# Inverse deviations of the norms taken by GpSimd as a power, in a conv, attention and expert-routing kernel

## What is computed

```python
def _gn(v, G=32, eps=1e-05):          # over pairs of channels and all pixels
    ...
    return ((g - m) / jnp.sqrt(s + eps)).reshape(v.shape)
def _ln_t(v, eps=1e-05):              # over the 64 channels of a token
    ...
    return (v - m) / jnp.sqrt(s + eps)
...
x = x + _L0_conv_ref(_gn(x), ...)     # depthwise 5x5 taps, 1x5 taps, correlations
t = _to_tokens(x)
t = t + _L1_attn_ref(_ln_t(t), ...)   # k features, k'v matrices, q features, denominators
t = t + _L1_ffn_ref(_ln_t(t), ...)    # softmax over tokens, 8 tokens per expert, gelu network
```

## Time and profile before

| | us |
|---|---|
| median of 3 runs | 4081.96 (4072.59 to 4082.1) |
| the profiled execution | 4079.0 |
| its span, first to last instruction | 4077.2 |
| PE, DVE, ACT, POOL busy | 3586.0, 2994.3, 1687.9, 1248.6 |

### The profile page before, as it was taken

How to read it: one execution, slowest core, us unless ns; L and a number is a source line. 1 busy time by engine, 2 the same in 40 slices (tenths; PEclk the granted TensorE clock), 3 DMA queues, 4 the chain that set the end, 5 groups by cost and what they waited for, 6 DMA issues and landing times.

```text
span 4077.2 us, 52073 instructions
## 1 busy us (share of the span) xinstructions
PE 3586.0 (88%) x17556; PEld 1798.3 (44%) x17556; DVE 2994.3 (73%) x3523; ACT 1687.9 (41%) x1798; POOL 1248.6 (31%) x1327
## 2 busy tenths in 40 slices
PE   4798998989889998989889899899989898899976
PEld 2344444444544444444444445344444444544453
DVE  6878876788677876788767886778767887548823
ACT  0145533455254534445434553445435554343310
POOL 1015620176013740156201760127501572011100
PEclk8899998999999998999989999999989999899967
DMA  1000000000000001000000000000010000100045
GB/s 47 17 1 1 1 17 25 1 1 1 25 17 1 1 1 41 1 1 1 17 25 1 1 1 25 17 1 1 1 41 1 1 1 16 30 1 1 1 116 200
DMA packets 18676, 70.96 MB, mean 17 GB/s; under 512 B 8781, under 2 KB 13421, under 8 KB 13485
## 3 DMA queue, kind: packets, MB, share of 16 engines
q1 hardware_dynamic: 18365, 67.10, 5.3%
HBM read 37.26 MB, written 29.84 MB: 16 GB/s over the span
## 4 chain that ended last, share of the span: by engine, by line
issue 48%; PE 33%; DVE 8%; POOL 7%; ACT 2%; DMA 1%; SPq 1%; POOLq 0%; DVEq 0%; ACTq 0%
PE ps_D L1499 11%; POOL UA L549 4%; PE ps_E L1463 4%; PE ps_C L1488 3%; PE ps_A L1446 3%; PE ps_B L1446 3%; DVE RR L1106 2%; PE ps_E L1474 1%; DVE region L1076 1%; DVE arena L911 1%; PE ps_C L1417 1%; POOL RS L581 1%; PE ps_E L1512 1%; POOL RR L574 1%; DVE region L1085 1%
## 5 line engine op out<-in xcount | busy, mean ns | idle before, releaser
L562 POOL TENSOR_TENSOR arena<-arena,UHL 128x896 f32<-128x896 f32 x350 | 764.6, 2210 | 226.3 <-ACT UHL L695 211.6
L1499 PE MATMUL ps_D<-region,small 128*128 128x448 f32 x1792 | 785.2, 562 | 32.9 <-DVE OS L1112 32.8
L549 POOL TENSOR_TENSOR UA<-region,CS 128x128 f32<-128x128 f32 (+1 forms) x400 | 178.8, 449 | 1837.8 <-DVE region L986 795.3
L1085 DVE TENSOR_TENSOR region<-region,ps_C 128x896 f32<-128x896 f32 x448 | 485.9, 1085 | 247.9 <-PE ps_C L1488 247.9
L1499 PEld LDWEIGHTS ps_D<-region,small 128*128 128x128 f32 x1792 | 321.2, 194 | 346.7 <-issue 284.8
L734 ACT ACTIVATE EQ<-ps_B,NEG 128x896 f32<-128x896 f32 x224 | 225.6, 1007 | 480.4 <-PE ps_B L1446 480.3
L911 DVE SCALAR_TENSOR_TENSOR arena<-arena,W8C 128x896 f32<-128x896 f32 (+1 forms) x418 | 416.8, 1010 | 1.2
L1417 PE MATMUL ps_C<-region,UA 128*128 128x512 f32 (+1 forms) x800 | 382.7, 601 | 2.9 <-ACT region L627 2.9
L734 ACT ACTIVATE EQ<-ps_A,NEG 128x896 f32<-128x896 f32 x224 | 225.6, 1007 | 350.8 <-PE ps_A L1446 350.7
L695 ACT ACTIVATE UHL<-arena,W8C 128x896 f32<-128x896 f32 x350 | 361.2, 1032 | 0.0
L1052 DVE SCALAR_TENSOR_TENSOR region<-region,ps_B 128x1024 f32<-128x1024 f32 (+1 forms) x200 | 243.9, 1219 | 159.8 <-ACT region L713 156.4
(11 more groups left out here) (310 smaller groups left out, 5772.9 us busy)
## 6 DMA issues: line engine op xcount, KB each, us to landing
arena<-x SPq DMA_DIRECT2D x8, 1568.0 KB, 6.6
t_keep<-Y SPq DMA_DIRECT2D x7, 1568.0 KB, 6.8
w_keep<-region SPq DMA_DIRECT2D x7, 784.0 KB, 5.7
CST<-t_keep SPq DMA_DIRECT2D x2, 1568.0 KB, 10.0
small<-t_keep SPq DMA_DIRECT2D x2, 1568.0 KB, 12.8
plane<-w_keep SPq DMA_DIRECT2D x4, 784.0 KB, 15.9
UHL<-t_keep SPq DMA_DIRECT2D x2, 1568.0 KB, 12.3
out<-CST SPq DMA_DIRECT2D x2, 1568.0 KB, 11.7
```

The source lines that it names most:

```text
L562: pool.tensor_tensor(out=X[:, cut], in0=X[:, cut], in1=PRODUCT[m % 3], op=ALU.add).then_inc(pool_taps.sem, 1)
L1085: dve.tensor_tensor(out=q, in0=q, op=ALU.mult, in1=here.area(key)[:, :].rearrange("p (c n) -> p c n", c=2)[:, :, 0:PIX])\
L1499: ins = pe.matmul(here.area(key)[:, 0:PIX], MW[i][:, c, :], Q[s % 3][:, c, :], start=c == 0, stop=c == NCHUNK - 1)
```

## The change

The power of minus one half of (variance + epsilon) takes the place of root and reciprocal. For each token group POOL does two instructions on 14 columns (`deviations`: multiply by 1/64 and add epsilon, then a power whose exponent is a column of -0.5), with a wait of its own between them. For the channel norm DVE adds epsilon out of PSUM at tile 16 (`SPREAD_TILE`), POOL takes the power of one column behind its `UA` of that tile, and `NORM_TILE` goes from 16 to 18. ACT's roots and DVE's reciprocals of deviations are gone (DVE's self-waits from 53 to 44 a pass), and with them all table loads but those of the first instruction and of the last function. Tiles are moved: the power for groups 2 and 3 at tiles 5 and 9, scaling at 7 and 11 (from 9 and 10), split at 8 and 12 (from 11 and 12), transposes at 11 and 15 (from 13 and 15). In the slots the scaling is seven slots behind `LN2_SLOTS` instead of six. POOL's part of the two groups in `back` stands at the end of its pass.

```diff
-STD_TILE = 8
-SCALE_TILES = [None, None, 9, 10]
-SPLIT_TILES = [None, None, 11, 12]
-UTS_TILES = [None, 2, 13, 15]
+STD_TILES = [None, None, 5, 9]
+SCALE_TILES = [None, None, 7, 11]
+SPLIT_TILES = [None, None, 8, 12]
+UTS_TILES = [None, 2, 11, 15]
...
-STATS_TILE, MEAN_TILE, CENTRE_TILE, VAR_TILE, NORM_TILE = 3, 12, 13, 15, 16
+STATS_TILE, MEAN_TILE, CENTRE_TILE, VAR_TILE, SPREAD_TILE, NORM_TILE = 3, 12, 13, 15, 16, 18
...
+            def deviations(sums, std, pair, g, turn):
+
+                pool.wait_ge(*sums.at(pair, g + 1))
+                passed(pool)
+                pool.tensor_scalar(ST[:, g % 2, 2, :], ST[:, g % 2, 1, :], 1.0 / C, LN_EPS, ALU.mult, ALU.add)\
+                    .then_inc(variance.sem, 1)
+                pool.wait_ge(*turn)
+                pool.tensor_tensor(out=ST[:, g % 2, 3, :], in0=ST[:, g % 2, 2, :], op=ALU.pow,
+                                   in1=NEGH[:, 0:1].broadcast_to([P, 2 * GROUP])).then_inc(std.sem, 1)
+
+            def group_norm(here):
+
+                pool.wait_ge(*here.emptied("gvar"))
+                pool.tensor_tensor(out=MV[:, 7:8], in0=MV[:, 6:7], in1=NEGH[:, 0:1], op=ALU.pow)\
+                    .then_inc(gn_scale.sem, 1)
...
+                    if k in STD_TILES:
+                        deviations(ln1_sums, ln1_std, pair, STD_TILES.index(k), variance.at(pair, STD_TILES.index(k) - 1))
+                    if here.span == "loop" and k == SPREAD_TILE:
+                        group_norm(here)
...
-
+                    if j - 5 in LN2_SLOTS:
+                        deviations(ln2_sums, ln2_std, pair, LN2_SLOTS[j - 5], variance.at(pair, 3 + LN2_SLOTS[j - 5]))
+                deviations(ln2_sums, ln2_std, pair, NG - 1, variance.at(pair, 2 + NG))
+                for g in range(2) if here.span == "loop" else ():
+                    deviations(ln1_sums, ln1_std, pair + 1, g, variance.at(pair, 3 + NG + g))
...
-            def deviations(sums, std, pair, g):
-                act.wait_ge(*sums.at(pair, g + 1))
-                act.activation(ST[:, g % 2, 2, :], ST[:, g % 2, 1, :], ACT.Sqrt, scale=1.0 / C,
-                               bias=EPS[:, 0:1])\
-                    .then_inc(std.sem, 1)
...
-                    if k == VAR_TILE and here.span == "loop":
-                        group_norm(here)
...
-            def group_norm_apply(here):
-                dve.wait_ge(*here.emptied("gvar"))
-                link(dve.reciprocal(MV[:, 7:8], MV[:, 6:7]))
+            def group_norm_spread(here):
+                dve.wait_ge(*here.filled("gvar"))
+                dve.tensor_scalar(MV[:, 6:7], here.area("gvar")[:, 0:1], GN_EPS, None, ALU.add)\
+                    .then_inc(*here.empty("gvar"))
+
+            def group_norm_apply(pair):
+                dve.wait_ge(*gn_scale.at(pair, 1))
...
                 dve.wait_ge(*std.at(pair, g + 1))
-                link(dve.reciprocal(st[:, 3], st[:, 2]))
...
-                    if j - 6 in LN2_SLOTS:
-                        norm_scale(2, ln2_std, pair, LN2_SLOTS[j - 6]).then_inc(un2_ready.sem, 1)
+                    if j - 7 in LN2_SLOTS:
+                        norm_scale(2, ln2_std, pair, LN2_SLOTS[j - 7]).then_inc(un2_ready.sem, 1)
```

More of the change, by code:

```diff
@@ L200, in program @@
         GBC = sb("GBC", [C, 1])
-        EPS = sb("EPS", [P, 1])
         NEG1 = sb("NEG1", [P, 1])
+        NEGH = sb("NEGH", [P, 1])
         BS = sb("BS", [P, NPIX, 6])
@@ L343, in program @@
         gn_mean = signal("gn_mean", 1)
+        gn_scale = signal("gn_scale", 1)
+        variance = signal("variance", 2 * NG, setup=2)
         g_ready = signal("g_ready", 1)
@@ L526, in _ @@
             pool.memset(SEL[:, :, :, :, :], 0.0)
-            pool.memset(EPS[:, :], GN_EPS)
             pool.memset(NEG1[:, :], -1.0)
+            pool.memset(NEGH[:, :], -0.5)
             pool.memset(BD[:, :, :], 0.0)
@@ L584, in split @@
                     passed(pool)
-                for j in range(SLOTS + POOL_LAG):
+                for j in range(ALL_SLOTS):
                     if slot_of_step(j, RECIP_LAG + 1):
@@ L590, in pair_of_images @@
                         tap_sum(j - POOL_LAG)
+                    if j - 5 in LN2_SLOTS:
[3 more added lines that the diff above has]
+                    deviations(ln1_sums, ln1_std, pair + 1, g, variance.at(pair, 3 + NG + g))
+            group_norm(Here("setup"))
+            for g in range(2):
+                deviations(ln1_sums, ln1_std, 0, g, variance.first(g + 1))
             with pool.Fori(0, PAIRS - 1) as pair:
@@ L602, in _ @@
             act.wait_ge(*loaded.first(1))
[L604 to L608, removed]
             def front(here, chunks):
@@ L676, in back @@
                         split_tokens(here, 0)
-                    deviations(ln1_sums, ln1_std, pair, g)
                     high_part(pair, g)
@@ L716, in pair_of_images @@
                         tokens(here, 1, YT_TILES.index(k))
-                    if k == STD_TILE:
-                        for g in (2, 3):
-                            deviations(ln1_sums, ln1_std, pair, g)
                     if k in SPLIT_TILES:
@@ L740, in pair_of_images @@
                         tokens(here, 2, LN2_SLOTS[j])
-                    if j - 5 in LN2_SLOTS:
-                        deviations(ln2_sums, ln2_std, pair, LN2_SLOTS[j - 5])
                     if here.span == "loop" and j in FRONT_SLOTS:
                         front(here, [FRONT_SLOTS[j]])
-                deviations(ln2_sums, ln2_std, pair, NG - 1)
                 for g, (t, m) in enumerate(GROUPS):
@@ L763, in _ @@
             act.wait_ge(*zeroed.first(2))
-            group_norm(start)
             front(start, range(NPIX))
@@ L1139, in pair_of_images @@
                         group_norm_variance(here)
+                    if conv and k == SPREAD_TILE:
+                        group_norm_spread(here)
                     if conv and k == NORM_TILE:
-                        group_norm_apply(here)
+                        group_norm_apply(pair + 1)
                     if conv and k > NORM_TILE:
@@ L1182, in _ @@
             group_norm_variance(start)
-            group_norm_apply(start)
+            group_norm_spread(start)
+            group_norm_apply(0)
             back(start, 0, None)
@@ L1623, in _ @@
                         .then_inc(*end.fill(key))
-VSETUP = 63
-VLOOP = 53
+VSETUP = 60
+VLOOP = 44
 LOW = -3.0e38
```

## The result

| | us |
|---|---|
| before, median of 20 runs | 4079.37 (4069.91 to 4083.7) |
| after, median of 20 runs | 4102.35 (4076.03 to 4104.87) |
| ratio after / before, 95% interval | 1.0037, 1.0023 to 1.0051 |
| ratio of the two medians | 1.0056 |

The forecast was 4069, faster. The median lies inside its range of 4044 to 4108, but the sign is wrong. The two ratios in the table differ because the runs of after lie in two groups and the median falls into the larger. There is nothing between the groups: 8 of 20 at 4076.0 to 4079.1, 12 at 4101.9 to 4104.9. The profiled execution of after (4104.4, span 4102.6) is one of the longer.

What follows compares the result with a forecast made beforehand. PE, busy 88% of the span, was taken as the bound, with ACT mattering only where PE or DVE waits. Terms -40 + 19 + 10 - 2 = -13 us against 4079.0 gave 4066, 4069 for the median; range 4044 to 4108.

Steps and rivals of the forecast that it cites:

- the price of the power: POOL's power on 14 columns in the token norms: taken as 0.7 us, between 0.1 and 2.21.
- a serial place: One of 24 norms with nothing beside them: 0.8 us more each (bounds 0.1 and 2.5), 19 us in all.
- Rival (a): Power is slow software and the 24 serial places decide: at 2.1 us a power, 53 us and 4103; chance 0.23.
- Rival (b): Power costs like a product, at most 0.2 us: 0.3 us a serial norm, 7 us, giving 4057; chance 0.17.
- The sign to look for: End of the back stage: 1.4 us from sum to scaling, not 0.64; PE's next-pass wait longer by twice the difference.
- The k tiles: PE's waits around tiles 9 to 19 go: gain of about 40 us (bounds 25 and 47).
- Rival (c): K tiles broken in a new place by DVE's backlog at tile 7 or tile 11's copies: 4085; chance 0.10.
- the transposes' new place: Transposes at tile 11 remove both waits before tile 14: 3.4 us in two passes, 4.2 in five, 1.6 in the last.
- the missing exchange: At tile 8, no more table loads and roots on ACT between two exponentials: gain of 0.8 us a pass.
- The rule on the table load: Skill's drain of about 1.38 us per ACT load, 2.66 in all: tile 8's exchange would be 5.8 us, not 3.13.
- The moved pieces: Two depthwise pieces a pass move from k tiles into q slots 35 and 36: 1.5 us in seven passes, 10 us lost.
- An unchanged q stage gives 10 us back.: Sign against the forecast: if the q slots do not lengthen, the 10 us charged for the moved depthwise pieces return.

Runs made afterwards that it cites:

- run 7: Changed kernel with POOL's two instructions on 8 columns instead of 14 for the last group: 4101.18 us, ratio 1.0019 to the kernel before.
- the long form: The slower of two groups of runs of the unaltered changed kernel: 12 of 20 at 4101.9 to 4104.9 us; its profiled execution took 4104.4.
- the short form: The faster group of runs of the unaltered changed kernel, 8 of 20 at 4076.0 to 4079.1 us; profiled once more at 4078.0, span 4076.1.
- run 3: Kernel before with only the change's new tile numbers, roots and reciprocals kept everywhere: 4035.42 us, ratio 0.9890.
- run 5: Changed kernel with the power on POOL everywhere but the old tile numbers (powers at tiles 5 and 8): 4119.54 us, ratio 1.0052 to the kernel before.
- run 6: Kernel before with DVE's depthwise pieces beginning two tiles later, so two pieces a pass move into the q slots: 4085.14 us, ratio 0.9985.
- the hybrid: Changed kernel with ACT's root and DVE's reciprocal back in the 24 serial places, POOL's power kept elsewhere: 4023.31 us, ratio 0.9862 to the kernel before.

## Why the prediction was wrong

**The step that failed is the price of the power.** "I take 0.7, half as much again as the 128-column row, which is the nearest in size." It is 2.58. The size of a tile was the wrong yardstick: the rows of POOL then at hand were sums, products and casts, where 896 columns took 2.21 us, 0.0025 a column; run 7 gives the power 0.16 a column. The upper bound, 2.21, was drawn from the same kind of row and was also too low. The other terms of the chain were near: hand-overs 0.3 for 0.5, scale and add 0.21 for 0.2. With 2.58 in place of 0.7 a serial place costs 2.46 by the trace, 24 of them 59 and not 19, and my sum would have read -40 + 59 + 10 - 2 = +27, 4109. By stages the 24 places cost 54 us where 19 were forecast. That takes back the whole gain of the k tiles and leaves the change at nothing; that the median is slower beyond this is a second term, the long form's clock in the back stage, which the sum had at nothing without a reason.

Rival (a), with its break-even at a power of about 1.2 us, was the mechanism; it had a chance of 0.23. That its 4103 meets the median is luck: the k tiles gave 9 us more than its sum has, the q slots were not longer, the power cost more still, and 26 us in the back stage belong to the clock; the short form lies at 4078. That the median lies inside the range is luck of the same kind. The range itself was not added up right: the terms of a serial place give 0.2 to 2.3 us and not 0.1 to 2.5, so 5 to 55 us, and ends of 4045 and 4105.

Rival (b) priced the power at 0.2 us at most, a thirteenth of what it took. The Trainium skill's rule beside it (GPSIMD Engine Reference, Performance versus the Vector engine: about twice VectorE's time for two-input operations, measured there on an add) does not carry over: for this operation the trace does not agree, 2.58 us against the 0.5 worked out from it. The sign to look for, PE's wait ahead of the next pass longer by twice the difference, was misplaced too: half of it fell on the wait for the low part of group 0, and of the other half 0.98 went into slower matmuls.

**The k tiles: right in mechanism, 9 us short.** Forecast -40, measured -48.7 (-45.3 in the short form). Exponential 14 comes 2.58 us after 13 and no PE wait is left at tiles 12 to 14. In pairs two and five of the loop, k tiles go from 147.1 to 142.0, 5.1 us for the 4.7 forecast. In the other five it is some 149.2 to 142.0, 7.2 for 5.5. Part of that difference is clock. Busy time in 3.4 us ahead of exponential 14, before, pair three and then pair two:

```profile
1178.90:1182.30 3.40, 3.04 (x6) 1.45 (x7) 0.00 (x0) 1.35 (x2) 0.00 (x0) 0.51 0.00 0
705.90:709.30 3.40, 3.40 (x13) 1.67 (x12) 1.22 (x1) 1.11 (x1) 0.40 (x1) 1.00 0.00 0
```

In pair two too PE had just stood idle, but its clock stayed; in the five other passes it fell to the lower level for 3.4 us (6.8 in the first). In after it doesn't do so anywhere between the first three k tiles and the q slots. I had read the 7.62 of the earlier trace rows as a longer wait. Rival (c), tiles broken in a new place, didn't come.

**Who earned it.** I ascribed most of the gain to the transposes' new place and 0.8 a pass to the missing exchange. Runs 3 and 5 bear that out from both sides. That most of the 50 us of loads had been hidden was right as well: ACT is 138 us less busy, and in run 5 the missing roots are worth about 0.9 us of a pass. The rule on the table load that the prediction cites from the Trainium skill (ScalarE: Activation LUTs, What ACT_TABLE_LOAD costs) does not agree with one more exchange either: 3.13 us from tiles 8 to 9 in the earlier trace rows, 2.92 in run 3 with one root (685.20 to 688.12), where the two loads alone would be 5.3 by it.

**The moved pieces: the local price right, its part in the whole not found.** 1.5 us was forecast for the four slots; 1.7 and 0.9 were measured, and the q slots of run 6 are 10.8 us longer. By its runs the kernel before gets no slower by it all the same; where the loss is made up is open.

**"An unchanged q stage gives 10 us back."** It came out at -5.3 in after and +1.2 in the short form.

**What the sum didn't contain.** The clock in the back stage, +25.9 in after and -9.5 in the short form, is as large as any term of mine. In the short form all terms are -45.3 (k), +1.2 (q), +17.2 (drain), -9.5 (back), +33.4 (residuals), +1.9 (setup), together -1.1, the measured 4076.1 - 4077.2.

**Still open.** Why two executions of one kernel settle into one form or the other, and why the hybrid's four runs never showed the long form. What is seen is only that within a profile of after the passes two to seven are alike to 0.15 us. I tried no kernel that shifts the back stage by idleness alone.

## What to carry to other kernels

Before work is given to another engine, list the places where nobody has anything else to do: there the whole duration of the new operation counts, and one price that no row shows, times 24, took back the whole gain. Give an idle engine the same operation only where other work lies beside it, and keep the short one on the serial chain; even beside other work a gain from it was not shown here. A change like this should be split place by place, and its reordering tried by itself, since here the order of tiles alone was worth 1.1%. Where a kernel repeats one pass many times, compare the granted clock of the same stretch in every pass before ascribing a few us a pass to instructions.

## What the runs showed of the hardware

- POOL's power on float32 takes 0.55 us for 1 column of 128 partitions, 1.64 for 8 and 2.58 for 14; multiply-and-add on 14 columns takes 0.21, and VectorE's reciprocal on 14 takes 0.24.
- The hand-over DVE to POOL took 0.19 us (646.49 to 646.68), POOL's wait for itself 0.09, POOL to DVE 0.03.
- One kernel has two timings that recur, 4078 and 4103 us, 16 of 32 runs in each. In the traces they differ by where in each pass the granted clock of TensorE is at its lower level: the 50 pooling matmuls took 5.93 or 10.16 us, the 56 behind them 5.57 or 7.81.
